# Joining levels 32 and 64 of a triangular inverse by small TensorE tiles ahead of a gated delta-rule recurrence

## The chip, the cores and the metric

The kernel runs on one core of one Trainium2 chip. The metric is the device time of one execution in microseconds (us): 2207.28 us is the median of three runs of the kernel before (2204.56, 2207.28 and 2207.43 us). TensorE is called PE here, its weight loads PEld, VectorE is DVE, ScalarE is ACT, GpSimd is POOL, SyncE is SP.

## What is computed

The reference is one decoder block on x of shape 4 x 512 x 512: a gated delta-rule attention with 16 heads of width 128, a cross attention and a routed low-rank feed-forward. The change is in the first of the three. Its core, cut to what matters:

```python
qkv = silu(causal_depthwise_conv(layernorm(x) @ Wqkv))   # 4 taps
q, k = l2norm(q), l2norm(k)
def step(M, inp):                      # M: a 128 x 128 state per batch and head
    q_t, k_t, v_t, b_t, g_t = inp
    M = M * exp(g_t)
    M = M + outer(k_t, (v_t - k_t @ M) * b_t)
    return M, q_t @ M                  # scanned over the 512 tokens
out = rmsnorm(out) * norm_w * silu(z) @ Wout
```

The kernel doesn't step through tokens. It takes chunks of 128 tokens. In a chunk, the corrections of all tokens are the solution of a system with a unit triangular 128 x 128 matrix, I + N, where N is strictly triangular and holds the products of keys with their decays. The output and the next state follow from this solution by plain matrix products. The change concerns how I + N is inverted and applied.

## The kernel before, in words

There are 16 heads, processed one after the other (the first and the last are unrolled, the 14 between are a loop). For each head there are 4 batches (B) and 4 chunks (NC), so 16 independent 128 x 128 systems. All five engines run one instruction stream each, in the order in which the code is written; semaphores are the only coupling. There is no scheduler.

A head goes through these stages on PE:

1. decays, transposes of k, and the gram products k k^T (L563 to L588);
2. the projections of q and z as 12 products of 128 x 512 each, "jobs" (L515), and the transposes of v and q;
3. the products k q^T (L635);
4. the inverse. The 16 x 16 diagonal blocks are inverted by POOL (`blkT`), and come back through DRAM into `t32`; DVE transposes them to `tT`. Then pairs of blocks are merged: with T the block diagonal inverse so far and X the off-diagonal blocks of N at that level, the update is T := T - T X T. It takes two products per system: `merge_y` (L670, X against T), a copy of its result from PSUM by ACT (L1086), `merge_z` (L683), and a subtraction by DVE (L1388). Level 0 goes from 16 to 32 and is followed by a 32 x 32 block transpose into `t32` (L1391). Level 1 goes from 32 to 64 and takes its X from `x1`, which ACT fills (L1024). Each level is four groups (one per chunk) of `merge_y` and four of `merge_z`, and a group is 4 matrix products of 128 x 128, one for each batch. A float32 product of this kind is two MATMUL records in the trace;
5. the recurrence over the chunks c = 0 to 3. The last level, 64 to 128, is never formed. It is applied: `w1` = T r (L708), `vv` = X2 w1 (L714), T vv (L719), and w = w1 - T vv by DVE (L1408). ACT copies in between (L1100, L1108). Then come the state product (L728) and the output products (L734, L735). For c > 0 there is first a product of the state with the keys (L702), which DVE subtracts from the right hand side (`nv`, L1400).

Into the waits of stage 5, `ahead(count)` puts products of the next head's first seven jobs (K for four batches, V for three), one 128 x 512 product each, by the table `FILL`: rows are chunks, columns are the places after L702, L708, L714 and L719. Two of the seven jobs are done before stage 4, the other 60 products are in `FILL`. Each finished job is scaled by ACT (`tap`, L954) and convolved by DVE in three steps (L1316), and a job may only begin when the convolution of the job before it in the same PSUM bank has ended. The convolution of V of batch 1 stands in DVE's order in chunk 3, ahead of `normalise` (L1328), whose result PE transposes (L554).

The last head has no next head; `ahead` does nothing there. ACT and DVE instead split the output weights in each chunk (L1128, L1429).

## Time and profile before

| | us |
|---|---|
| median of 3 runs | 2207.28 |
| span of the profiled execution | 2206.9 |
| PE busy | 2103.0 (95%) |
| PEld busy | 1734.9 (79%) |
| DVE busy | 1242.6 (56%) |
| ACT busy | 988.4 (45%) |
| POOL busy | 814.4 (37%) |
| mean granted TensorE clock | 0.989 |

The span runs from the first to the last instruction; the time of this execution around its span is not listed separately, and the span is 0.4 us under the median. A busy share of PE is not a share of its peak: matmuls are pipelined, so the duration of one record (277 ns for a 128 x 128 one) is longer than the distance from one to the next. Distances are read from the starts of groups in the timeline.

### The profile page before, as it was taken

The page shows a single profiled execution, that of the slowest core. Times are in us where ns is not written, and L with a number is a line of the kernel's source. Part 1 is how long each engine was busy: PE and PEld are TensorE (multiplying, and loading weights), DVE is VectorE, ACT ScalarE, POOL GpSimd, SP SyncE. Part 2 cuts the span into 40 slices and gives each one's busy share as a digit, 9 for nine tenths or more (in the row PEclk, how much of TensorE's full clock was granted, in tenths as well). Part 3 has the DMA queues.
Part 4 walks back from the last instruction along what each step waited for, and adds up shares of the span by engine and source line. Part 5 has one row for each costly group of instructions (what it writes and reads, how often), then busy time and mean ns, then how long its engine had stood idle before and what let it go on. Part 6 is the DMA issues. An engine that isn't in the chain of part 4 may idle for free.

```text
span 2206.9 us, 37731 instructions
## 1 busy us (share of the span) xinstructions
PE 2103.0 (95%) x12418; PEld 1734.9 (79%) x12418; DVE 1242.6 (56%) x2160; ACT 988.4 (45%) x3083; POOL 814.4 (37%) x1169
## 2 busy tenths in 40 slices
PE   5899999999999999999999999999999799999999
PEld 4688888888988888888888888888898665757574
DVE  5656565656666656566565656565666544343434
ACT  2455454546364646454555545464636331212111
POOL 2254453535353636353545445353535200000000
PEclk9899999999999999999999999999999989999999
DMA  2011111101010101010101111111102340403020
GB/s 93 15 34 26 29 36 21 31 21 35 22 38 14 38 19 38 14 38 15 37 21 31 29 24 36 21 31 21 36 21 63 125 128 10 115 16 109 19 57 19
DMA packets 220091, 85.37 MB, mean 39 GB/s; under 512 B 138320, under 2 KB 204240, under 8 KB 219280
## 3 DMA queue, kind: packets, MB, share of 16 engines
q1 hardware_dynamic: 220048, 84.83, 15.2%
q8 instruction: 23, 0.38, 0.1%
q14 instruction: 20, 0.16, 0.0%
HBM read 57.28 MB, written 27.53 MB: 38 GB/s over the span
## 4 chain that ended last, share of the span: by engine, by line
PE 72%; issue 12%; DVE 9%; ACT 3%; POOL 2%; DMA 1%; POOLq 0%; DVEq 0%; SPq 0%; ACTq 0%
PE bank L515 27%; PE bank L683 5%; PE bank L670 5%; PE bank L771 4%; PE bank L708 3%; PE bank L635 3%; PE bank L728 2%; PE bank L735 2%; PE bank L714 2%; PE bank L719 2%; PE bank L734 2%; PE bank L702 2%; DVE vT L1316 2%; PE bank L588 1%; PE bank L834 1%
## 5 line engine op out<-in xcount | busy, mean ns | idle before, releaser
L515 PE MATMUL bank<-x_hi,w_hi 128*128 128x512 f32 x1024 | 422.6, 413 | 18.3 <-DVE w_lo L1263 11.6
L515 PE MATMUL bank<-x_hi,w_lo 128*128 128x512 f32 x1024 | 409.5, 400 | 0.0
L515 PE MATMUL bank<-x_lo,w_hi 128*128 128x512 f32 x1024 | 408.5, 399 | 0.0
L515 PEld LDWEIGHTS bank<-x_hi,w_hi 128*128 128x128 f32 x1024 | 194.0, 189 | 60.0 <-issue 16.2
L515 PEld LDWEIGHTS bank<-x_hi,w_lo 128*128 128x128 f32 x1024 | 193.8, 189 | 36.7
L515 PEld LDWEIGHTS bank<-x_lo,w_hi 128*128 128x128 f32 x1024 | 194.5, 190 | 31.3
L1316 DVE SCALAR_TENSOR_TENSOR qT<-bank,cw,qT 128x511 f32<-128x511 f32 (+2 forms) x192 | 143.4, 747 | 82.7 <-ACT qT L954 78.1
L1316 DVE SCALAR_TENSOR_TENSOR vT<-bank,cw,vT 128x511 f32<-128x511 f32 (+2 forms) x192 | 143.2, 746 | 44.8 <-ACT vT L954 40.3
L1707 POOL TENSOR_TENSOR o_rstd<-o_ms,minus_half 128x4 f32<-128x4 f32 x64 | 70.7, 1104 | 258.1 <-DVE o_ms L1395 258.1
L1739 POOL TENSOR_TENSOR rstd<-ve,mhalf 128x1 f32<-128x1 f32 x32 | 17.4, 543 | 387.6 <-DVE ve L1479 387.6
L1114 ACT ACTIVATE o_tmp<-bank 128x128 f32<-128x128 f32 x256 | 67.4, 278 | 201.5 <-PE bank L735 201.5
L1316 DVE SCALAR_TENSOR_TENSOR kT<-bank,cw,kT 128x511 f32<-128x511 f32 (+2 forms) x192 | 142.6, 743 | 8.6 <-ACT kT L954 4.1
L1666 POOL TENSOR_TENSOR x<-nT,upper 128x512 f32<-128x512 f32 x64 | 84.8, 1335 | 142.9 <-PE bank L670 142.9
L1712 POOL TENSOR_TENSOR state<-state,gam 128x512 f32<-128x512 f32 x32 | 33.6, 1050 | 275.9 <-PE bank L735 275.9
L683 PE MATMUL bank<-tT,y 128*128 128x128 f32 x1024 | 134.8, 277 | 0.5 <-DVE tT L1388 0.5
L1408 DVE TENSOR_TENSOR w<-w,bank 128x512 f32<-128x512 f32 x64 | 43.8, 685 | 159.3 <-PE bank L719 159.3
L670 PE MATMUL bank<-t,x 128*128 128x128 f32 x1024 | 133.3, 276 | 0.0
L670 PEld LDWEIGHTS bank<-t,x 128*128 128x128 f32 x1024 | 124.4, 192 | 1.2
L683 PEld LDWEIGHTS bank<-tT,y 128*128 128x128 f32 x1024 | 124.2, 192 | 0.8 <-issue 0.7
L1086 ACT ACTIVATE y<-bank 128x512 f32<-128x512 f32 x128 | 76.5, 598 | 105.8 <-PE bank L670 105.8
L1388 DVE TENSOR_TENSOR tT<-tT,bank 128x512 f32<-128x512 f32 x128 | 87.2, 681 | 50.6 <-PE bank L683 50.4
L771 PE MATMUL bank<-wo_hi,o_hi 128*128 128x512 f32 x256 | 105.3, 412 | 0.0
(219 smaller groups left out, 4860.6 us busy)
## 6 DMA issues: line engine op xcount, KB each, us to landing
w_raw<-in_w_heads SPq DMA_DIRECT2D x64, 256.0 KB, 2.8
o_d<-og SPq DMA_DIRECT2D x64, 256.0 KB, 2.6
o_raw<-o_d SPq DMA_DIRECT2D x16, 1024.0 KB, 6.1
x_in<-in_x SPq DMA_DIRECT2D x16, 256.0 KB, 3.4
blkN_d<-nT SPq DMA_DIRECT2D x64, 64.0 KB, 2.0
t<-blkT_d SPq DMA_DIRECT2D x64, 64.0 KB, 2.4
wo_raw<-in_w_out SPq DMA_DIRECT2D x4, 1024.0 KB, 7.9
x_res<-in_x SPq DMA_DIRECT2D x16, 256.0 KB, 2.7
```

What stands on the lines that cost most here:

```text
L515: last = mm(bank[bk][:, :], w[:, kind % 2, d, :], xx[:, d, b * S:(b + 1) * S], start=(n == 0), stop=(n == 3 * ND - 1))
L635: last = mm(grid(5 + 2 * (c % 2))[:, b, :], kT[:, b, c, :], qT[:, b, c, :], start=True, stop=True)
L670: last = mm(grid(3 + n % 2)[:, b, :], x, t32[:, b, c, :], start=True, stop=True)
L683: last = mm(grid(5 + 2 * (n % 2))[:, b, :], y1[:, n % 2, b, :], tT[:, b, c, :], start=True, stop=True)
L708: last = mm(grid(3)[:, b, :], tT[:, b, c, :], nv[:, b, c, :], start=True, stop=True)
L771: last = mm(bank[c % 2][:, :], o[:, c % 2, k, :], w[:, k, :], start=(n == 0), stop=(n == 3 * H - 1))
L1086: fn(y1[:, n % 2, :, :], grid(3 + n % 2), ACT.Copy).then_inc(y_copied, 1)
L1114: last = fn(o_tmp[:, b, :], grid(4)[:, b, :], ACT.Square, accum_out=o_sq[:, c, b:b + 1])
L1316: stt(d[:, k:S], bank[JOB_BANK[JOBS.index((kind, b))]][:, 0:S - k], cw[:, kind, TAPS - 1 - k:TAPS - k], d[:, k:S], ALU.mult, ALU.add).then ...
L1388: tt(tT[:, :, c, :], tT[:, :, c, :], grid(5 + 2 * (n % 2)), ALU.subtract).then_inc(merged, 1)
L1666: tt(x0[:, (c + 1) % 2, :, :], nT[:, :, c, :], upper[:, :].unsqueeze(1).to_broadcast([P, B, P]), ALU.mult).then_inc(x0_done, 1)
L1707: tt(o_rstd[:, c, :], o_ms[:, c, :], minus_half[:, 0:B], ALU.pow).then_inc(orstd_done, 1)
```

## The change

Level 1 of the merges (8 groups of full products per head) and the two applied products of the recurrence (`vv`, T vv) are taken out. In their place stands a piece between the merges and the recurrence that completes the inverse in `tT`:

- `join32_y`, `join32_z`: 32 x 32 products that make the 64 x 64 inverses. `join32_y` has 16 products for each half g (two chunks), `join32_z` 24: two for `tT`, and a third whose transposed result goes to `t32`. Two tiles of the array alternate in them (j = 0 and 1), with results in different PSUM banks.
- `join64_y`, `join64_z`: 64 x 64 products, 8 per half each, that make the upper right 64 x 64 block of the 128 x 128 inverse.
- Copies from PSUM by ACT after the y parts and of the third product, and by DVE after the z parts.

In all there are 80 products of 32 x 32 and 32 of 64 x 64 per head. The recurrence then applies `tT` once (L708 before) and waits for `inverse_done`. `JOIN_FILL` puts 12 products of the next head into the joins, and `FILL` now has two places per chunk and 48 products. POOL no longer clears blocks of `nT` but one block of `t32`; ACT's filling of `x1` goes.

```diff
-FILL = ((0, 4, 4, 4), (7, 4, 4, 1), (6, 4, 4, 2), (6, 4, 4, 2))
+FILL = ((0, 6), (7, 7), (7, 7), (7, 7))
+JOIN_FILL = (4, 2, 3, 3)
+EARLY, LATE = slice(0, P // 2), slice(P // 2, P)
+FRONT = [slice(2 * j * PAIR, 2 * j * PAIR + PAIR) for j in range(2)]
+BACK = [slice(2 * j * PAIR + PAIR, 2 * j * PAIR + 2 * PAIR) for j in range(2)]
...
-    MERGES = 2 * NC
+    MERGES = NC
+    def front_bank(g, j):
+        return 3 + (g + j) % 2
+    def back_bank(g, j):
+        return 5 + 2 * ((g + j) % 2)
+    def half_bank(g):
+        return (2, 6)[g]
...
+                def join32_y(g):
+                    pe.wait_ge(t32_done, 4 * h + 2 * g + 2)
+                    pe.wait_ge(y_copied, MERGES * h + MERGES)
...
+                    for i in range(2):
+                        for b in range(B):
+                            for j in range(2):
+                                c = 2 * g + i
+                                last = mm(small(front_bank(g, j), BACK[j], i, b), nT[FRONT[j], b, c, BACK[j]],
+                                          t32[FRONT[j], b, c, FRONT[j]], start=True, stop=True)
+                    last.then_inc(y32_mm, 1)
+                def join32_z(g):
+                    pe.wait_ge(y32_done, 2 * h + g + 1)
+                    pe.wait_ge(merged, MERGES * h + MERGES)
...
+                            for j in range(2):
+                                mm(small(back_bank(g, j), FRONT[j], i, b), y32[BACK[j], c, b, :], tT[BACK[j], b, c, BACK[j]],
+                                   start=True, stop=True)
+                            last = mm(small(back_bank(g, 0), BACK[0], i, b), tT[BACK[0], b, c, BACK[0]], y32[BACK[0], c, b, :],
+                                      start=True, stop=True)
+                    last.then_inc(z32_mm, 1)
+                def join64_y(g):
+                    pe.wait_ge(z32n_done, 2 * h + g + 1)
...
+                            last = mm(large(half_bank(g), LATE, i, b), nT[EARLY, b, c, LATE], t32[EARLY, b, c, EARLY],
+                                      start=True, stop=True)
+                    last.then_inc(y64_mm, 1)
+                def join64_z(g):
+                    pe.wait_ge(y64_done, 2 * h + g + 1)
+                    pe.wait_ge(z32_done, 2 * h + g + 1)
...
+                            last = mm(large(half_bank(g), EARLY, i, b), y64[LATE, c, b, :], tT[LATE, b, c, LATE],
+                                      start=True, stop=True)
+                    last.then_inc(z64_mm, 1)
+                join32_y(0)
+                ahead(JOIN_FILL[0])
+                join32_y(1)
+                join32_z(0)
+                ahead(JOIN_FILL[1])
+                join32_z(1)
+                join64_y(0)
+                ahead(JOIN_FILL[2])
+                join64_y(1)
+                join64_z(0)
+                ahead(JOIN_FILL[3])
+                join64_z(1)
...
-                    pe.wait_ge(merged, MERGES * h + NC + c + 1)
+                    pe.wait_ge(inverse_done, 2 * h + c // 2 + 1)
...
                     last.then_inc(w1_mm, 1)
                     ahead(fill[1])
-                    pe.wait_ge(w1_done, 4 * h + c + 1)
-                    pe.wait_ge(x2_only, 2 * h + 2)
-                    for b in range(B):
-                        last = mm(grid(2)[:, b, :], nT[:, b, c, :], w1[:, c % 2, b, :], start=True, stop=True)
-                    last.then_inc(v_mm, 1)
-                    ahead(fill[2])
-                    pe.wait_ge(vv_done, 4 * h + c + 1)
-                    for b in range(B):
-                        last = mm(grid(3)[:, b, :], tT[:, b, c, :], vv[:, b, :], start=True, stop=True)
-                    last.then_inc(tv_mm, 1)
-                    ahead(fill[3])
...
+                def keep32_y(g):
+                    act.wait_ge(y32_mm, 2 * h + g + 1)
...
+                    for j in range(2):
+                        last = fn(y32[BACK[j], 2 * g:2 * g + 2, :, :], smalls(front_bank(g, j), BACK[j]), ACT.Copy)
+                    last.then_inc(y32_done, 1)
+                def keep32_n(g):
+                    act.wait_ge(z32_mm, 2 * h + g + 1)
+                    fn(t32[BACK[0], :, 2 * g:2 * g + 2, FRONT[0]].rearrange("p b c s -> p c b s"),
+                       smalls(back_bank(g, 0), BACK[0]), ACT.Copy, scale=-1.0).then_inc(z32n_done, 1)
+                def keep64_y(g):
...
                 for c in range(NC):
                     act.wait_ge(w1_mm, 4 * h + c + 1)
-                    fn(w1[:, c % 2, :, :], grid(3), ACT.Copy).then_inc(w1_done, 1)
+                    fn(w1[:, c % 2, :, :], grid(3), ACT.Copy).then_inc(w_done, 1)
                     if more and c == 3:
                         tap(h + 1, V_, 1)
...
-                    fn(vv[:, :, :], grid(2), ACT.Copy).then_inc(vv_done, 1)
...
+                def join32(g):
+                    dve.wait_ge(z32_mm, 2 * h + g + 1)
...
+                def join64(g):
+                    dve.wait_ge(z64_mm, 2 * h + g + 1)
+                    ts(tT[EARLY, :, 2 * g:2 * g + 2, LATE].rearrange("p b c s -> p c b s"), larges(half_bank(g), EARLY),
+                       -1.0, None, ALU.mult).then_inc(inverse_done, 1)
...
-                    dve.wait_ge(tv_mm, 4 * h + c + 1)
-                    tt(w1[:, c % 2, :, :], w1[:, c % 2, :, :], grid(3), ALU.subtract).then_inc(w_done, 1)
```

PE's order shows the two places of which the prediction speaks. The first is the start of the joins in the loop over the heads. Before, from the first `merge_y` of level 1 on, with the `merge_z` of one chunk behind each (`x_95` is `x1`, `y_96` is `y1`, `t_91` is `t32`):

```order
L670 MATMUL bank<-t_91,x_95 128x128 x4
L675 REGISTER_ALU
L683 MATMUL bank<-tT,y_96 128x128 x4
L670 MATMUL bank<-t_91,x_95 128x128 x4
L675 REGISTER_ALU
L683 MATMUL bank<-tT,y_96 128x128 x4
L670 MATMUL bank<-t_91,x_95 128x128 x4
L675 REGISTER_ALU
L683 MATMUL bank<-tT,y_96 128x128 x4
L670 MATMUL bank<-t_91,x_95 128x128 x4
L675 REGISTER_ALU
L683 MATMUL bank<-tT,y_96 128x128 x4
```

In the changed kernel the same place on PE, from the last `merge_y` (L701, `x_107` is `x0`) and the last two `merge_z` (L712) on; `y_104` is `y32`:

```order
L701 MATMUL bank<-t_91,x_107 128x128 x4
L712 MATMUL bank<-tT,y_96 128x128 x8
L733 MATMUL bank<-t_91,nT 32x32 x16
L570 ISA
L552 MATMUL bank<-x_hi,w_hi 128x512
L552 MATMUL bank<-x_lo,w_hi 128x512
L552 MATMUL bank<-x_hi,w_lo 128x512
L552 MATMUL bank<-x_hi,w_hi 128x512
L733 MATMUL bank<-t_91,nT 32x32 x16
L738 ISA
L748 MATMUL bank<-tT,y_104 32x32 x2
L750 MATMUL bank<-y_104,tT 32x32
```

Runs of small tiles and runs of full ones take turns: PE goes from one shape to another 11 times in a head with a next one (into `join32_y(0)`, into and out of each of the four fills, from 32 to 64 at `join64_y(0)`, and into the recurrence).

The second place is chunk 3 of the recurrence in the same loop. Before, from L708 to L719; two more L515 follow, and then the transposes L554 of the normalised output of chunk 2:

```order
L708 MATMUL bank<-nv,tT 128x128 x4
L515 MATMUL bank<-x_hi,w_lo 128x512
L515 MATMUL bank<-x_hi,w_hi 128x512
L515 MATMUL bank<-x_lo,w_hi 128x512
L515 MATMUL bank<-x_hi,w_lo 128x512
L714 MATMUL bank<-w_97,nT 128x128 x4
L515 MATMUL bank<-x_hi,w_hi 128x512
L515 MATMUL bank<-x_lo,w_hi 128x512
L515 MATMUL bank<-x_hi,w_lo 128x512
L515 MATMUL bank<-x_hi,w_hi 128x512
L719 MATMUL bank<-vv,tT 128x128 x4
```

And in the changed kernel, where L807 is what L708 was and L591 what L554 was:

```order
L807 MATMUL bank<-nv,tT 128x128 x4
L552 MATMUL bank<-x_hi,w_lo 128x512
L552 MATMUL bank<-x_hi,w_hi 128x512
L552 MATMUL bank<-x_lo,w_hi 128x512
L552 MATMUL bank<-x_hi,w_lo 128x512
L552 MATMUL bank<-x_hi,w_hi 128x512
L552 MATMUL bank<-x_lo,w_hi 128x512
L552 MATMUL bank<-x_hi,w_lo 128x512
L591 MATMUL bank<-ident,o_tmp 128x128 x4
```

Between these two, PE now has 7 fills; before it had 10 and two groups of full products. The orders of ACT (copy of `w1`, tap of V of batch 1, then tap of batch 2) and of DVE (`nv`, mean square, convolution of V of batch 1, `normalise`) in chunk 3 are as before but for the removed copy and subtraction.

## Rows read from the trace of the kernel before

**Rows 1.** Page: busy time of each engine, and the ending chain by engine

```profile
PE 2103.0 (95%) x12418; PEld 1734.9 (79%) x12418; DVE 1242.6 (56%) x2160; ACT 988.4 (45%) x3083; POOL 814.4 (37%) x1169
...
PE 72%; issue 12%; DVE 9%; ACT 3%; POOL 2%; DMA 1%; POOLq 0%; DVEq 0%; SPq 0%; ACTq 0%
```

**Rows 2.** Ending chain in order of time, two heads: start, us, what

```profile
902.05 0.93 PE bank L515 x4
...
928.39 0.23 PE bank L563
...
1033.18 0.23 PE bank L563
```

**Rows 3.** Timeline of PE, one head: start, us, instructions, idle before

```profile
985.29 1.06 PE L670 MATMUL bank<-t,x 128*128 128x128 f32 x8
986.18 1.06 PE L683 MATMUL bank<-tT,y 128*128 128x128 f32 x8
...
993.39 1.06 PE L708 MATMUL bank<-nv,tT 128*128 128x128 f32 x8
...
999.08 1.15 PE L728 MATMUL bank<-w,k_tok 128*128 128x128 f32 x8
...
1001.01 1.16 PE L702 MATMUL bank<-state,kdT 128*128 128x128 f32 x8
...
1003.83 1.16 PE L708 MATMUL bank<-nv,tT 128*128 128x128 f32 x8
...
1020.21 1.16 PE L728 MATMUL bank<-w,k_tok 128*128 128x128 f32 x8
...
1022.99 1.06 PE L702 MATMUL bank<-state,kdT 128*128 128x128 f32 x8
...
1025.27 1.05 PE L708 MATMUL bank<-nv,tT 128*128 128x128 f32 x8
...
1030.54 0.66 PE L554 MATMUL bank<-ident,o_tmp 128*128 128x128 f32 x4
...
1032.94 0.48 PE L563 MATMUL bank<-gt,after_r 128*128 128x512 f32 x1
```

**Rows 4.** Timeline of PE in the tail: full weights against 8 columns

```profile
1849.16 0.96 PE L831 MATMUL bank<-wg_sb,xfT 128*128 128x8 f32 x8
1849.97 2.39 PE L834 MATMUL bank<-a_sb,xfT 128*128 128x512 f32 x5
```

**Rows 5.** Timeline of DVE, the same head

```profile
1021.49 0.69 DVE L1418 TENSOR_TENSOR state<-state,bank 128x512 f32<-128x512 f32 x1 [0.45 <-PE bank L728]
1022.10 2.31 DVE L1316 SCALAR_TENSOR_TENSOR vT<-bank,cw,vT 128x511 f32<-128x511 f32 x3
...
1027.57 2.32 DVE L1316 SCALAR_TENSOR_TENSOR vT<-bank,cw,vT 128x511 f32<-128x511 f32 x3 [2.49 <-ACT vT L954]
1029.80 0.68 DVE L1328 TENSOR_TENSOR o_tmp<-bank,o_rstd 128x512 f32<-128x512 f32 x1
```

**Rows 6.** Timeline of ACT, the same head

```profile
986.88 0.61 ACT L1024 ACTIVATE x<-nT 32x128 f32<-32x128 f32 x2
...
1026.36 0.60 ACT L1100 ACTIVATE w<-bank 128x512 f32<-128x512 f32 x1 [0.98 <-PE bank L708]
1026.85 0.68 ACT L954 ACTIVATE vT<-bank,cw 128x512 f32<-128x512 f32 x1
```

**Rows 7.** Timeline of PE and ACT, last head

```profile
1721.34 1.06 PE L708 MATMUL bank<-nv,tT 128*128 128x128 f32 x8
...
1726.87 1.16 PE L728 MATMUL bank<-w,k_tok 128*128 128x128 f32 x8 [0.78 <-DVE w L1408]
...
1730.11 1.92 ACT L1128 ACTIVATE wo_hi<-wo_raw 128x2048 fp32r<-128x2048 f32 x1
...
1736.38 1.16 PE L728 MATMUL bank<-w,k_tok 128*128 128x128 f32 x8 [0.34 <-DVE w L1408]
```

**Rows 8.** Windows: one stretch with PE busy time, mean clock (PEclk)

```profile
1849.10:1850.10 1.00, 1.00 (x12) 1.00 (x10) 0.82 (x3) 0.91 (x2) 0.00 (x0) 1.00 0.00 0
```

More of the change, by code:

```diff
@@ new lines, in join32_z @@
+                def join32_z(g):
+                    pe.wait_ge(y32_done, 2 * h + g + 1)
+                    pe.wait_ge(merged, MERGES * h + MERGES)
+                    if g and not more:
+                        pe.wait_ge(z32_done, 2 * h + 1)
+                        pe.wait_ge(z32n_done, 2 * h + 1)
+                    hold(pe, "pe")
+                    for i in range(2):
+                        for b in range(B):
+                            c = 2 * g + i
+                            for j in range(2):
[4 more added lines that the diff above has]
+                    last.then_inc(z32_mm, 1)
```

157 lines of the change are left out of this document (83 added, 74 removed).

## The prediction

> **What bounds the kernel now.** I read the page first: PE is busy for 95% of the span, and 72% of the chain that ended last is PE's own work [rows 1]. So time taken from PE's stream counts, as long as no other engine becomes late. Then the chain in order of time gives the period: one head from L563 to L563 takes 104.8 us [rows 2], and 15 heads have a next head to fill in. One filled product costs 0.23 us (four in 0.93) [rows 2]. Then the timeline of PE through one head: a merge group starts 0.89 us after the one before it, so a full 128 x 128 float32 record takes 0.111 us of PE (8 in a group), though its duration reads longer [rows 3]. Last, DVE and ACT in chunk 3, where they are barely on time for PE [rows 5, 6].
>
> **The change, part by part, for a head with a next one.**
>
> (a) Level 1 of the merges goes. From the first level-1 group to L708 of chunk 0 there are 8.10 us [rows 3], and one group of 0.89 (the last `merge_z` of level 0) stays: minus 7.2 us.
>
> (b) The recurrence loses `vv` and T vv, two groups of about 0.92 with their hand-over, so 1.84 per chunk, and 12 fills of 0.23. What becomes late next decides how much of this is real.
> - Chunk 0: L708 to L728 takes 5.69 us now [rows 3]. Without 1.84 and six fills (1.38) it is 2.3 with ACT's copy (0.60) hidden by the fills: minus 3.4.
> - L728 of chunk 0 to L708 of chunk 1 is 4.75 us [rows 3]. DVE sets it (state copy, convolution, `nv`) and it stays.
> - Chunks 1 and 2 lose 1.84 each, and one and two fills net: minus 2.4 and minus 2.2. In the latter the last job must wait for DVE's convolution after the state sum: 0.61 + 2.31 after the sum begins, which is 1.28 after L728 [rows 3, 5], so at 4.2. PE has got there at 0.99 + 1.79 + 0.9 + 0.5 = 4.1 (L728 to L702 is 2.78 [rows 3]). A wait of 0.1.
> - Chunk 3 gains nothing. L708 to L554 takes 5.27 us [rows 3]. The path is not PE's: L708 to its end 1.06, ACT's copy, ACT's tap, DVE's convolution of 2.32, `normalise` of 0.68, then L554 [rows 3, 5, 6]. None of these moves. PE now has 0.85 + 7 x 0.23 = 2.5 us of work there, so it stands idle for 2.8 us where it had been covered by 1.84 + 0.69 more. L554 to the next head is 2.40 as before [rows 3].
>
> Sum: from L708 of chunk 0 to the next head 39.55 us now [rows 3], minus 3.4, 2.4 and 2.2: 31.5, minus 8.0 us.
>
> (c) The joins are added: 80 products of 32 x 32 and 32 of 64 x 64, two records each, so 160 and 64 records. No row has such a tile. The nearest is L831: 8 columns move, the loaded weights are 128 columns, and it still takes 0.81 us for 8 records, 0.10 each [rows 4], no less than with 128 columns. So the weight load sets the full-size record, and it could shrink with the columns: 28 ns (a quarter of 111) and 56 ns (half) are the lower bounds, and 111 ns is the upper bound for both, if a record costs the same whatever its tile. I take 50 ns for the small, between the bounds, nearer the lower since two tiles alternate, and 58 ns for the medium, close to the row scaled by its columns: 160 x 0.050 = 8.0 and 64 x 0.058 = 3.7.
>
> (d) Twelve fills move here: 2.8 us. Covers: ACT's two copies of 32 x 256 cost some 0.65 us (two of 32 x 128 took 0.61 [rows 6]); four fills (0.93) or a z part lie beside each. The first wait that is not covered is `join32_y(1)` for the last transpose on DVE: 0.1 us, and 0.7 if the small tiles are at their lower bound.
>
> (e) Eleven changes of tile shape. No row has one. Below: nothing. Above: the array runs empty, which is the duration of a 128 x 128 record less its distance; a group of 8 shows 1.06 for 0.89 [rows 3], so 0.17 each, 1.9. I take 0.07 each, 0.8, since a run of small tiles can begin beside the end of a full one.
>
> (f) Off the path: ACT loses `x1`, POOL its two memsets for a small one, DVE four subtractions in the merges and four in the recurrence. ACT and DVE take short PSUM reads instead. None of it is where PE waits. Nothing.
>
> Per head: minus 7.2, minus 8.0, plus 8.0 + 3.7 + 2.8 + 0.1 + 0.8 = 15.4, so plus 0.2 us; 15 heads: plus 3.
>
> **The last head** has no fills. Its joins are exposed: 8.0 + 3.7, 0.8 for the shapes, and a wait of about 1 us for copies, 13.5 against 7.2: plus 6.3. The recurrence gains more than elsewhere, since nothing covered the two copies: L708 to L728 was 5.53 [rows 7] and becomes 1.75 (1.06, 0.60 and two hand-overs). Between L728 of chunks 0 and 1 lay 9.5 [rows 7]; what remains is the output product, squares, ACT's split of 1.92 [rows 7] and the copy, 5.7: minus 3.8. The next two gain 3.5 each, with DVE's split of the output weights then near the path. Minus 14.6; net minus 8.
>
> Total: plus 3 minus 8 on a span of 2206.9 gives 2202; I say 2201 us, as the third figures don't carry. The median is 0.4 above the span, which changes nothing.
>
> **A rule against the change.** Nothing in these rows drains PE for a new shape. The Trainium skill, "TensorEngine Tiling (Array Packing)", Key Properties, says that a change of the tiling mode drains the engine, while tiles of one mode work in parallel. No row here shows either. The first is the third rival below, the second the first.
> The same page (Instruction Overhead) gives a matmul a cost of about 60 cycles however few columns it has. At 2.4 GHz that would be an estimate of 25 ns for each of a record's passes, in place of 28 ns by columns.
>
> **Rivals.**
>
> 1. The alternating tiles overlap fully, and a record costs its columns: 28 and 56 ns, shapes free. 4.5 + 3.6 + 2.8 + 0.7 = 11.6 per head instead of 15.4; minus 3.6 a head, minus 55, and minus 11 in the last: 2141 us. For it: distinct banks and partitions for j = 0 and 1. Against: only the 32 x 32 parts alternate.
>
> 2. A record costs nearly as much as a full one (fetching, starting and loading it), at the upper bound 111 ns: 160 and 64 of them are 24.9 us in place of 11.7. Plus 13.4 a head: some 2415. A related one: such thin work lets the granted clock fall. L831 ran at 1.00 with 8 columns [rows 8], but for under a microsecond. If the joins ran at half clock, their 11.7 and the fills' 2.8 would double: plus 14.5 a head, 2430; for half of the stretch, 2315.
>
> 3. The slower side, as one mechanism: at each change of shape PE runs empty and also can't load the new weights ahead. 0.17 for the drain and as much again for the load make 0.35; eleven are 3.9 in place of 0.8. Plus 3.1 x 16 = 50: 2251 us. It decides from 0.13 us per change on: 0.06 x 11 x 16 = 10.6 eats the 6 us and 0.2% more.
>
> 4. PE is not short of 2.8 us in chunk 3, if the tap of V there starts before ACT's copy. The order of ACT speaks against it. Minus 2.8 x 15 = 42: 2159.
>
> **How the numbers follow.** Forecast 0.31 (its own range 2180 to 2225, since 10 ns on the small record is 1.6 us a head, 26 in all), overlap 0.27, changes of shape 0.23, dear records or clock 0.16, chunk 3 0.03. Within 0.2% (4.4 us, about what a measurement can tell from no change) lies a third of the forecast: 0.10. Faster: 0.15 of the forecast, 0.27, 0.03 and a little of the others: 0.46. Slower: the rest, 0.44. The range for 8 in 10 runs from the overlap to the half-slow clock: 2140 to 2310.
>
> **What would show it.** In the changed profile: starts of the groups of 32 x 32, divided by 32 or 48 records (1.6 and 2.4 us expected; 0.9 and 1.3 by rival 1; 3.6 and 5.3 by rival 2). The distance from the last small record to the first fill against that inside a run (rival 3). The granted clock of the stretch. PE idle before the transposes of chunk 2's output in chunk 3, waiting for DVE's `normalise`, 2.8 us in each of 15 heads. From w1 of chunk 0 to the next head 31.5 us. I am wrong if a small record is outside 40 to 60 ns, if a change of shape takes over 0.13 us, or if that idle time is missing.

## The result, and the profile of the changed kernel

| | before | changed |
|---|---|---|
| median, us | 2207.02 (4 runs) | 2134.25 (4 runs, 2129.81 to 2136.12) |
| ratio, with 95% interval | | 0.967 (0.9656 to 0.9684) |
| profiled execution / its span | - / 2206.9 | 2134.65 / 2132.9 |
| mean granted TensorE clock | 0.989 | 0.980 |
| one head to the next, us | 104.7 mean | 99.4 in the shortest, 100.1 mean |

The changed kernel is 3.3% faster. The forecast was 2201 us, 0.3% faster, and its range ended at 2140. Its sign was right and its size was not.

The lines have moved: L563 is now L600, L515 is L552, L708 is L807, L728 is L817, L702 is L801, L554 is L591, ACT's `tap` L954 is L1043, DVE's convolution L1316 is L1404 and `normalise` L1328 is L1416. L733 is `join32_y`, L748 and L750 are `join32_z`, L764 is `join64_y`, L775 is `join64_z`.

The page (busy time by engine, then the ending chain by engine), to be held against [rows 1]:

```profile
PE 1988.0 (93%) x13954; PEld 1619.9 (76%) x13954; DVE 1201.4 (56%) x2128; ACT 928.9 (44%) x2955; POOL 790.2 (37%) x1152
...
PE 65%; issue 15%; DVE 15%; ACT 2%; POOL 2%; DMA 1%; DVEq 0%; POOLq 0%; ACTq 0%; SPq 0%
```

PE has 1536 records more and is busy for 115 us less. The chain has shifted from PE (72% to 65%) towards DVE and "issue": PE now waits at some places.

The joins of one head in PE's timeline (start, us, instructions, idle before). They stand where [rows 3] had the level-1 merges:

```profile
1046.26 2.01 PE L712 MATMUL bank<-tT,y 128*128 128x128 f32 x16
1048.20 0.69 PE L733 MATMUL bank<-t,nT 32*32 32x32 f32 x32
1048.82 0.50 PE L552 MATMUL bank<-x_hi,w_hi 128*128 128x512 f32 x1
...
1050.25 0.60 PE L733 MATMUL bank<-t,nT 32*32 32x32 f32 x27 [0.23 <-DVE t L1477]
...
1051.32 0.50 PE L552 MATMUL bank<-x_lo,w_hi 128*128 128x512 f32 x1
...
1052.61 1.14 PE L764 MATMUL bank<-t,nT 64*64 64x64 f32 x16
1053.68 0.50 PE L552 MATMUL bank<-x_hi,w_hi 128*128 128x512 f32 x1
...
1054.58 0.97 PE L764 MATMUL bank<-t,nT 64*64 64x64 f32 x13
...
1056.41 0.50 PE L552 MATMUL bank<-x_hi,w_hi 128*128 128x512 f32 x1
...
1057.30 1.14 PE L775 MATMUL bank<-tT,y 64*64 64x64 f32 x16
1058.37 1.16 PE L807 MATMUL bank<-nv,tT 128*128 128x128 f32 x8
```

Read the distances, not the durations. Thirty-two small records take 0.62 us (1048.20 to 1048.82). The next run of 80 takes 1.07 (1050.25 to 1051.32), and the last of 48 0.63 (1051.98 to 1052.61). That is 2.32 us for 160 records, 14 ns each, where 50 ns were forecast and 28 was the lower bound. The 64 medium records take 1.07, 1.83 and 1.07 us (the three rows of L764 and L775 with the next row's start), 62 ns each. Three fills take 0.90 (1053.68 to 1054.58) where three distances of 0.23 make 0.69, so each of the two changes of shape around them costs 0.10 at most, and less if the runs of small tiles give some of it back. With 0.1 taken off for the change at the end of each run, the small record is 13 ns and the medium 57. From the first small record to L807 there are 10.2 us.

The recurrence after it runs from L807 at 1058.37 to the next head's L600 at 1089.42 in the same timeline, 31.05 us. The end of it, as PE and then DVE show it (timelines of chunk 3, to be held against [rows 3, 5]); the first fence is PE one head earlier, the second DVE:

```profile
987.85 0.63 PE L591 MATMUL bank<-ident,o_tmp 128*128 128x128 f32 x4 [2.66 <-issue]
...
990.02 0.48 PE L600 MATMUL bank<-gt,after_r 128*128 128x512 f32 x1
```

```profile
1084.23 2.32 DVE L1404 SCALAR_TENSOR_TENSOR vT<-bank,cw,vT 128x511 f32<-128x511 f32 x3 [2.95 <-ACT vT L1043]
1086.47 0.68 DVE L1416 TENSOR_TENSOR o_tmp<-bank,o_rstd 128x512 f32<-128x512 f32 x1
```

PE stands idle for 2.66 us before L591, behind the convolution and `normalise`, as forecast (2.8). The waits of PE over the whole span (us, times, longest):

```profile
PE bank L591 <- issue: 42.2, 18, 2.7
```

Something was not forecast: after that idle time the clock falls. The head that begins at 688.06, again PE's timeline, and the windows (length, PE busy, PEld, DVE, ACT, POOL, clock, DMA, GB/s):

```profile
685.18 0.63 PE L591 MATMUL bank<-ident,o_tmp 128*128 128x128 f32 x4 [2.66 <-issue]
...
688.06 0.77 PE L600 MATMUL bank<-gt,after_r 128*128 128x512 f32 x1
```

```profile
688.00:692.00 4.00, 4.00 (x21) 3.43 (x21) 2.36 (x5) 3.53 (x15) 1.99 (x4) 0.75 0.24 66
990.00:994.00 4.00, 4.00 (x27) 3.48 (x26) 2.89 (x6) 3.67 (x17) 2.11 (x4) 1.00 0.22 66
```

The same L600 reads 0.77 us at one head and 0.48 at another. In the slower one the granted clock was 0.50 (1.2 GHz) for some 3 us. This happens behind 8 of the 15 idle times of 2.66 us; the fall begins while PE is still idle or up to 1.4 us after it has gone on. Before, every head start had 1.00.

Where the time went, from the starts of the heads: 15 periods were 1570.5 us and are 1501.7, minus 68.7. Fifteen times the shortest period (99.37) would be 1490.6, so a gain of 79.9 was there and some 11 of it is given back by the clock. The part ahead of the first head is 2.0 shorter, which need not be the change's doing: that part varies between 89.2 and 91.6 us over the kernels of this document. The part from the last head's start on is 3.4 shorter. The sum is minus 74.1 on the span.

### The profile page after: what moved, and what is told of

It is laid out like the page before. It is cut to its first block, busy times and chain, and to the rows that moved or that the text cites. A ratio compares the mean times of both kernels' runs of the same rounds, so it can differ in the third digit from the quotient of the medians.

```text
span 2132.9 us, 40248 instructions
## 1 busy us (share of the span) xinstructions
PE 1988.0 (93%) x13954; PEld 1619.9 (76%) x13954; DVE 1201.4 (56%) x2128; ACT 928.9 (44%) x2955; POOL 790.2 (37%) x1152
## 4 chain that ended last, share of the span: by engine, by line
PE 65%; issue 15%; DVE 15%; ACT 2%; POOL 2%; DMA 1%; DVEq 0%; POOLq 0%; ACTq 0%; SPq 0%
PE bank L552 28%; PE bank L860 4%; DVE kT L1404 3%; PE bank L807 3%; PE bank L672 3%; PE bank L824 3%; PE bank L823 2%; DVE t L1477 2%; PE bank L801 2%; PE bank L817 2%; DVE tT L1475 2%; DVE tT L1466 2%; PE bank L764 2%; PE bank L775 2%; PE bank L625 1%
## 5 line engine op out<-in xcount | busy, mean ns | idle before, releaser
L552 PE MATMUL bank<-x_hi,w_hi 128*128 128x512 f32 x1024 | 425.1, 415 | 20.2 <-DVE w_lo L1351 11.9
L552 PE MATMUL bank<-x_lo,w_hi 128*128 128x512 f32 x1024 | 404.9, 395 | 0.0
L552 PE MATMUL bank<-x_hi,w_lo 128*128 128x512 f32 x1024 | 404.9, 395 | 0.0
L552 PEld LDWEIGHTS bank<-x_hi,w_hi 128*128 128x128 f32 x1024 | 193.0, 188 | 70.8 <-issue 16.4
L552 PEld LDWEIGHTS bank<-x_hi,w_lo 128*128 128x128 f32 x1024 | 192.7, 188 | 39.8
L552 PEld LDWEIGHTS bank<-x_lo,w_hi 128*128 128x128 f32 x1024 | 193.5, 189 | 31.4
L1404 DVE SCALAR_TENSOR_TENSOR qT<-bank,cw,qT 128x511 f32<-128x511 f32 (+2 forms) x192 | 143.4, 747 | 83.4 <-ACT qT L1043 78.9
L1404 DVE SCALAR_TENSOR_TENSOR vT<-bank,cw,vT 128x511 f32<-128x511 f32 (+2 forms) x192 | 143.2, 746 | 51.5 <-ACT vT L1043 47.0
L1404 DVE SCALAR_TENSOR_TENSOR kT<-bank,cw,kT 128x511 f32<-128x511 f32 (+2 forms) x192 | 142.6, 743 | 7.9 <-ACT kT L1043 3.4
L860 PE MATMUL bank<-wo_hi,o_lo 128*128 128x512 f32 x256 | 99.9, 390 | 0.0
L860 PE MATMUL bank<-wo_lo,o_hi 128*128 128x512 f32 x256 | 99.9, 390 | 0.0
L1460 DVE TENSOR_TENSOR pT<-bank,pT 128x512 f32<-128x512 f32 x64 | 44.2, 691 | 98.6 <-PE bank L672 98.6
L1733 POOL TENSOR_TENSOR pT<-pT,cvec 128x512 f32<-128x512 f32 x64 | 67.1, 1049 | 85.2 <-DVE cvec L1435 82.4
L824 PE MATMUL bank<-w,pT 128*128 128x128 f32 x512 | 96.8, 288 | 0.0
L1194 ACT ACTIVATE w<-bank 128x512 f32<-128x512 f32 x64 | 38.2, 598 | 125.6 <-PE bank L807 125.5
L1351 DVE TENSOR_TENSOR w_lo<-w_raw,w_hi 128x512 fp32r<-128x512 f32 x64 | 53.5, 836 | 68.2 <-ACT w_hi L1019 68.2
```

The source lines that it names most:

```text
L552: last = mm(bank[bk][:, :], w[:, kind % 2, d, :], xx[:, d, b * S:(b + 1) * S], start=(n == 0), stop=(n == 3 * ND - 1))
L824: last = mm(grid(4)[:, b, :], pT[:, b, c, :], w1[:, c % 2, b, :], start=(c == 0), stop=True)
L860: last = mm(bank[c % 2][:, :], o[:, c % 2, k, :], w[:, k, :], start=(n == 0), stop=(n == 3 * H - 1))
L1351: tt(w_lo[:, kind % 2, :, :], w_raw[:, kind % 2, :, :], w_hi[:, kind % 2, :, :].bitcast(F32), ALU.subtract).then_inc(wlo_done, 1)
L1404: stt(d[:, k:S], bank[JOB_BANK[JOBS.index((kind, b))]][:, 0:S - k], cw[:, kind, TAPS - 1 - k:TAPS - k], d[:, k:S], ALU.mult, ALU.add).then ...
L1460: tt(pT[:, :, c, :], grid(5 + 2 * (c % 2)), pT[:, :, c, :], ALU.mult).then_inc(pT_done, 1)
```

## The experiments

Three theories were put to the test, each with its opposite. Overlap: the small record is cheap because two tiles take turns (against: it is cheap by its few columns alone). Clock: thin work by itself lowers the granted clock (against: only idle time does). Chunk 3: the idle time there comes from the order of work on ACT and DVE and can be taken away (against: something else holds PE up next). The letters in the expectations mean what each of them says.

### e3_one_tile: the same products, one tile after the other

```diff
-                    for i in range(2):
-                        for b in range(B):
-                            for j in range(2):
+                    for j in range(2):
+                        for i in range(2):
+                            for b in range(B):
```

`join32_z` is turned in the same way, its three kinds of product one after the other.

> The changed kernel with the 32 x 32 products in another order: all of one tile of the array, then all of the next, instead of alternating. The number of products is the same. Theory A (the 13 to 16 ns come from neighbouring tiles working at the same time; one tile alone takes its columns, 28 ns a record): 160 x 13 ns = 2.1 us a head more, 2134 + 33 = 2167 us at most, and runs of 32 records of L733 that last 0.9 us in place of 0.5. Rival B (a record of 32 columns costs 14 ns whatever its neighbour): 2134, runs as long as before.

Measured: 2265.54 us (2265.16 to 2265.97), ratio 1.0265 (1.0248 to 1.0282). PE's timeline, and three windows of 4 us from 905.30 on:

```profile
903.33 1.09 PE L733 MATMUL bank<-t,nT 32*32 32x32 f32 x32
904.36 0.50 PE L552 MATMUL bank<-x_hi,w_hi 128*128 128x512 f32 x1
...
909.88 1.97 PE L767 MATMUL bank<-t,nT 64*64 64x64 f32 x16
911.78 0.79 PE L552 MATMUL bank<-x_hi,w_hi 128*128 128x512 f32 x1
```

```profile
905.30:909.30 4.00, 4.00 (x119) 3.41 (x118) 0.83 (x2) 1.13 (x3) 0.00 (x0) 1.00 0.00 0
909.30:913.30 4.00, 4.00 (x41) 3.12 (x38) 0.83 (x2) 0.97 (x2) 0.00 (x0) 0.55 0.00 0
913.30:917.30 4.00, 4.00 (x35) 3.73 (x35) 0.60 (x1) 0.59 (x1) 0.52 (x1) 0.50 0.00 0
```

The first 32 records take 1.03 us in place of 0.62 at the same clock. Without the 0.1 for the change of shape behind them that is 29 ns each against 16. So the record is cheap because different tiles take turns. The total is not explained by it: the clock goes to 0.50 about 6 us into the joins and stays there for some 14 us, and all heads but the first take 108.4 to 109.3 us. The expectation had no term for that, and missed by 100 us.

### e2_small_twice and e4_medium_twice: each product issued twice

```diff
                         for b in range(B):
-                            for j in range(2):
...
+                            for _ in range(2):
+                                for j in range(2):
...
```

```diff
-                            last = mm(large(half_bank(g), LATE, i, b), nT[EARLY, b, c, LATE], t32[EARLY, b, c, EARLY],
-                                      start=True, stop=True)
+                            for _ in range(2):
+                                last = mm(large(half_bank(g), LATE, i, b), nT[EARLY, b, c, LATE], t32[EARLY, b, c, EARLY],
+                                          start=True, stop=True)
```

> The changed kernel with every 32 x 32 product issued twice in a row (160 records more per head; the second one writes the same result). Theory A (a small record costs 13 to 16 ns of PE, tiles overlapping): 2.1 to 2.6 us a head, less up to 0.5 that lies in the wait for DVE's last transpose: 2134 + 16 x 1.7 to 2.5 = 2161 to 2174 us. Rival B (50 ns each, as predicted, with the present gain from elsewhere): 2134 + 16 x 8 = 2262. Rival C (the records' time is hidden behind waits for ACT and DVE): no change, 2134.

> The changed kernel with every 64 x 64 product issued twice in a row (64 records more per head, 56 ns each by the starts in the trace). Theory A: 3.6 us a head, 2134 + 16 x 3.6 = 2191 us (somewhat more if the slow clock of the last head doubles it there). Rival (a record of the same tile behind another is cheaper since the weights are the same): under 2170.

Measured: medium twice 2196.72 us (2196.1 to 2201.35), 62.5 above the changed kernel. That is 3.9 us a head for 64 more records, 61 ns each, near the 58 of the forecast. The medium term stands. The last head, at its lower clock, is part of this mean; the shortest periods, 103.10 against 99.37, give 58.

Small twice took 2334.14 us (2333.56 to 2336.9), 200 above the changed kernel and far from every expectation. The record alone doesn't do it; in the timeline of the joins 64 of them run in 1.13 us, 18 ns each:

```profile
941.52 1.20 PE L734 MATMUL bank<-t,nT 32*32 32x32 f32 x64
```

A head takes 110 to 116 us. The clock is at 0.50 for 10 to 17 us of it, in and after the joins, and in most heads again around the head's start. Besides, PE waits with no releaser in the trace, among the small products (L750) and at the head's start (L619, and L600 with 8.3 us in 13 waits); together with one wait of 2.6 these make 53 us:

```profile
PE bank L750 <- issue: 23.5, 22, 1.7
PE bank L619 <- issue: 18.6, 13, 1.9
```

What these waits stand behind can be seen in the DMA queue that the page names "instruction": it holds 159 packets of 16 KB here and 26 in the changed kernel. This is taken up at e9_full_extra. How the 200 us divide between records, waits and clock was not measured one by one.

### e6_one_tile_filled: one tile, with more full products between the joins

Against e3_one_tile:

```diff
-FILL = ((0, 6), (7, 7), (7, 7), (7, 7))
-JOIN_FILL = (4, 2, 3, 3)
+FILL = ((0, 6), (6, 6), (6, 6), (6, 6))
+JOIN_FILL = (6, 4, 4, 4)
```

> The changed kernel with the 32 x 32 products one tile after the other (as in e3_one_tile) and 18 instead of 12 filled products in the joins (JOIN_FILL 6, 4, 4, 4; FILL 0, 6 and then 6, 6 three times). It tells apart the two costs in e3's extra 131 us. Theory A (28 ns a record for a tile by itself, 2.1 us a head; the rest of e3 was the granted clock, which fell in the joins because too little full-size work lay between the small runs): the clock stays at 1.00 and the time is 2134 + 33 + some 10 for waits in the chunks with fewer fills = 2165 to 2185. Rival B (the clock falls by the thin work itself, whatever lies between): 2250 or more, clock 0.93 as in e3.

Measured: 2211.34 us (2208.83 to 2211.83, 10 runs), ratio 1.0016 (1.0007 to 1.0026). It lies between the two expectations, 54 us below e3_one_tile. The joins now hold their clock in all 15 heads that have a next one, where e3_one_tile lost it in 14; the end of the head, of which six fills were taken away, does not. Windows of the joins (13.60 us) and of the end of the same head:

```profile
988.60:1002.20 13.60, 13.60 (x243) 11.41 (x242) 4.25 (x8) 3.44 (x8) 0.70 (x2) 1.00 0.00 0
```

```profile
1031.10:1035.10 4.00, 3.06 (x21) 3.09 (x21) 3.07 (x6) 0.00 (x0) 0.00 (x0) 0.77 0.04 12
```

PE's waits show what else the moved fills cost: 27.3 us in 32 waits for the convolution of k, which now is late in chunk 1.

```profile
PE bank L552 <- DVE kT L1407: 27.3, 32, 5.8
```

A head takes 104.95 us in the mean, against 100.1. Of these 4.8 some 2.1 are the order of the records, 1.4 is this wait, and 0.5 two shorter ones (for the convolution of V, and the idle time before L591, now 2.87). The clock falls at the end of 11 of the 15 heads in place of 8. Its share was not taken apart; it lies in the 0.8 that is left. What follows: with more full products among them the same small records, at the same cost, no longer lower the clock.

### e9_full_extra: nine more full products in the joins of the changed kernel

```diff
+                def extra(count):
+                    if more:
+                        pe.wait_ge(conv_done, 12 * (h + 1) + conv_index(K_, 1) + 1)
+                        for _ in range(count):
+                            mm(bank[1][:, :], w_hi[:, K_ % 2, 0, :], x_hi[:, 0, 0:S], start=True, stop=True)
                 join32_y(0)
+                extra(3)
                 ahead(JOIN_FILL[0])
```

Two more stand ahead of each of the other three `ahead`. Their results are not used.

> The changed kernel with nine more 128 x 512 products per head between the joins' small runs (in 15 heads, into a bank that is free there; nothing reads their result): 9 x 0.23 = 2.1 us a head, the same extra time as e3_one_tile's records, but full-width work. Theory A (e3's fall of the clock comes from thin work, not from a longer stretch): clock as in the changed kernel, 2134 + 15 x 2.1 less what lies in the 0.23 us wait = 2162 to 2168 us. Rival (a longer stretch of joins is what makes the clock fall): well over 2200.

Measured: 2181.03 us, with 10 runs from 2168.28 to 2204.2, ratio 0.9886 (0.9853 to 0.9918). The fastest run lies at the expectation's end; the median is 13 above it. The trace shows two things on top of nine products of 0.23 us. The clock falls at the head's start again (a head is 102.45 us, where 99.37 and 2.08 make 101.45), so full work in the joins doesn't guard against the idle time of chunk 3. In the joins of these heads it holds, so a longer stretch is not what lowered it in e3_one_tile. And at four heads PE waits for 1.7 to 3.5 us before the first product of a head, with no releaser:

```profile
506.20 0.76 PE L600 MATMUL bank<-gt,after_r 128*128 128x512 f32 x1 [3.48 <-issue]
```

That wait is neither in the kernel before nor in the changed one. In the kernel with the small products twice it is there as well. The traces show what goes with it. The queue named "instruction" on the page, of this kernel between 400 and 505 us and of e2_small_twice over the whole span (packets, MB, share):

```profile
q8 instruction: 9, 0.15, 0.7%
q8 instruction: 159, 2.61, 0.5%
```

In the changed kernel this queue brings 12 packets in the first two heads and then none until the end of the fifteenth. Here it goes on through the sixth head, and the four waits stand exactly at the starts of the third to the sixth; from 700 to 1600 us there is no packet and no such wait. In e2_small_twice and e12_norm_small_twice it brings 8 to 13 packets in every head, and every head has such waits: in e12, a packet is on its way from 370.94 to 372.11, and PE stands idle from 372.21 to 373.64. So these are waits of PE for its instructions, as far as the traces tell; no run took the packets away by themselves. Why the loop needs them again in these kernels is open: e4_medium_twice has more PE records in a head than this one, and no packet between its second head and its last two. The four waits are 11.0 us of this execution. Whether they are also the wide spread is not shown, since one execution was profiled.

### e1_tap_first: the tap of V ahead of the copy of w

In chunk 3, ACT reads the finished projection of V before it copies `w1`.

```diff
+                    if more and c == 3:
+                        tap(h + 1, V_, 1)
                     fn(w1[:, c % 2, :, :], grid(3), ACT.Copy).then_inc(w_done, 1)
-                    if more and c == 3:
-                        tap(h + 1, V_, 1)
```

> The changed kernel with one edit: in chunk 3 ACT does the tap of V of batch 1 ahead of its copy of w1. Theory A (PE's idle 2.66 us ahead of the transposes L591 in 15 heads is the chain w1 - ACT copy - tap - DVE convolution - normalise, and the falls of the granted clock at 8 of the head starts follow from that idle time): the idle time goes, the clock stays at 1.00 at every head start, the heads become 96.7 us long, 15 x 2.66 = 40 us plus some 11 us of slow clock: about 2084 us. Rival B (the clock falls because the small tiles are thin work): the idle time goes but the falls stay: about 2094. Rival C (another wait, POOL's or DVE's, takes the place at once): 2125 or more.

Measured: 2095.26 us (2093.96 to 2096.6), ratio 0.9491 (0.9475 to 0.9506), 39.0 less than the changed kernel. Heads take 97.4 us, all alike, and each begins at a clock of 1.00. The idle time before L591, of PE over the whole span:

```profile
PE bank L591 <- issue: 12.8, 18, 0.8
```

ACT, DVE and PE at that place, each from its timeline:

```profile
863.30 0.64 ACT L1019 ACTIVATE w_hi<-w_raw 128x512 fp32r<-128x512 f32 x1
863.83 0.70 ACT L1043 ACTIVATE vT<-bank,cw 128x512 f32<-128x512 f32 x1
```

```profile
864.56 2.32 DVE L1404 SCALAR_TENSOR_TENSOR vT<-bank,cw,vT 128x511 f32<-128x511 f32 x3 [0.99 <-ACT vT L1043]
```

The tap stands behind two other pieces of work of ACT (the silu of k and the split of w), so it comes at 863.83 and DVE still waits 0.99 for it. Fifteen times 1.97 us make 30, and with the clock's 11 that are no longer lost 41; 39 were measured. The expectation of 2084 had taken all of the idle time away; 0.71 of it stays. Behind that shorter idle time the clock falls in none of the 15 heads.

### e7_norm_first: and `normalise` ahead of the convolution

On top of e1_tap_first, in DVE's chunk 3:

```diff
+                        normalise(h, c - 1)
                         if more and c == 3:
                             conv(h + 1, V_, 1)
-                        normalise(h, c - 1)
```

> The changed kernel with two edits in chunk 3: ACT's tap of V of batch 1 ahead of its copy of w1 (as in e1_tap_first, 2095 us), and DVE's normalise of chunk 2 ahead of the convolution of that V. Theory: e1's remaining idle time of 0.71 us ahead of L591 is normalise behind the convolution; it goes, and nothing else moves up: 2095 - 15 x 0.7 = 2085 us. Rival (the convolutions end later, and DVE is late at the next head's start, at k_sqe and k_tok): 2095 or more.

Measured: 2081.54 us (2080.07 to 2082.99), ratio 0.9429 (0.9413 to 0.9445). Heads take 96.5 us, and no wait before L591 is left in them. PE's timeline in chunk 3, the seventh fill and what follows it:

```profile
859.99 0.39 PE L552 MATMUL bank<-x_hi,w_lo 128*128 128x512 f32 x1
860.21 0.60 PE L591 MATMUL bank<-ident,o_tmp 128*128 128x128 f32 x4
```

That is 3.5 us under the 2085 expected. From the chunk 3 idle time alone, the two edits take 2.8 us a head and the clock's fall: 52.7 us of 2134. The idle time is caused by the order in which ACT and DVE do their work, and is not needed.

### e11_norm_one_tile and e12_norm_small_twice: the clock without the idle time of chunk 3

On e7_norm_first, the edit of e3_one_tile and that of e2_small_twice:

```diff
...
-                            for j in range(2):
...
+                    for j in range(2):
...
```

```diff
...
+                            for _ in range(2):
...
```

> The kernel is e7_norm_first (2081.5 us, heads of 96.5 us, clock 1.00 at every head start) with the small products in the order of e3_one_tile. Two readings of e3_one_tile, which was 131 us slower than the changed kernel and lost its clock in the joins: (A) the thin one-tile joins lower the granted clock by themselves; then it falls here too, and the same 131 us come on top, 2190 to 2225 us, with a clock of 0.50 in the later part of the joins; (B) the clock fell only because PE had also stood idle in chunk 3 before, and without that idle time it stays at 1.00: then only the records cost more, 160 x 13 ns = 2.1 us per head, 33 us in all, 2105 to 2125 us. A at 0.55, B at 0.45.

> The kernel is e7_norm_first with each 32 x 32 product issued twice, as in e2_small_twice, which was 200 us slower than the changed kernel. (A) the thin joins lower the clock by themselves: again about 200 us on top, 2250 to 2300 us; (B) with no idle time in chunk 3 the clock holds: 160 more records at 14 ns, 2.2 us, and some 1.5 us of the waits without a releaser that e2_small_twice showed between the small products, 3.7 us per head, 60 us in all, 2125 to 2155 us. The z parts will show whether those waits (1.44 us at the longest) are there at full clock too.

Measured: one tile 2175.13 us (2172.64 to 2184.34), ratio 0.9868 (0.9845 to 0.989); small twice 2303.57 us (2293.66 to 2309.21), ratio 1.0426 (1.0394 to 1.0458).

For small twice, A's number nearly holds (its range ended 4 us lower): the clock falls in the joins of every head with a next one, for 10 to 17 us. It is not a test of A's reason, though, since PE waits with no releaser in the joins of each of these heads, for 1.2 to 1.7 us, and the fall comes 0.5 to 3.7 us after that wait begins.

One tile is the clean test: from 926 us to the end of the joins of that head no wait of PE over 0.03 us is in the trace. It lies between A and B, and its heads tell why. Seven of them take 97.4 to 98.65 us, eight take 106.0 to 106.1, nearly in turns. The short ones are 96.54 plus 2.08, which is B's price. That it is B's to the tenth is partly luck: the runs of small records are 2.4 us longer in these joins, 15 ns for each of 160, and some 0.3 of that lies in the wait of 0.23 before the second `join32_y`, which is gone. The long ones have the clock at 0.50 for about 17 us in and after the joins: A's fall, 7.45 us more. Eight times 7.45 and fifteen times 2.08 are 91 of the 94 measured. The windows of two heads in a row (868.00 in the first and 966.60 in the second are both 59.2 us behind the head's start):

```profile
868.00:872.00 4.00, 4.00 (x89) 3.14 (x87) 1.36 (x4) 1.88 (x5) 0.00 (x0) 1.00 0.00 0
872.00:876.00 4.00, 4.00 (x78) 3.48 (x78) 1.13 (x3) 0.97 (x2) 0.00 (x0) 1.00 0.00 0
...
966.60:970.60 4.00, 4.00 (x88) 3.14 (x88) 1.35 (x4) 1.88 (x5) 0.00 (x0) 1.00 0.00 0
970.60:974.60 4.00, 4.00 (x66) 3.82 (x65) 1.10 (x3) 0.37 (x1) 0.00 (x0) 0.54 0.00 0
974.60:978.60 4.00, 4.00 (x30) 3.25 (x30) 0.00 (x0) 1.02 (x2) 0.32 (x1) 0.50 0.00 0
```

PE's records fill these windows (4.00 of 4.00) where the clock falls. So the busy time of the profile doesn't tell whether the clock will hold; the same code holds it in one head and not in the next.

The Trainium skill, "TensorE: Matmul & The Clock Gate", HAM oscillation, ties a falling clock to waits between bursts of matmuls. The trace agrees in chunk 3, where the idle time of 2.66 us, shorter than the waits of the page's case, stands before the fall and its removal cures it. It doesn't agree in the joins of the one-tile kernel, where no wait stands before it.

In small twice the waits between small products come at full clock too, ahead of the fall. PE in the joins, where the window from 932.80 to 936.80 has a clock of 0.96:

```profile
934.46 0.22 PE L750 MATMUL bank<-tT,y 32*32 32x32 f32 x2 [1.44 <-issue]
```

### e10_best: the best version

On e7_norm_first, the convolution of k is moved between `join32` and `join64` on DVE, and the last head, which has no fills, gets full products in their place, with a result that is not used:

```diff
+                def keep_warm(count):
+                    if not more:
+                        for _ in range(count):
+                            mm(bank[0][:, :], ident[:, :], nT[:, 0, :, :], start=True, stop=True)
                 join32_y(0)
+                keep_warm(3)
                 ahead(JOIN_FILL[0])
```

Two, one and one of them stand at the other three places. On DVE `join64` has the moved convolution ahead of it:

```diff
-                    conv(h + 1, K_, 1)
...
+                if more:
+                    conv(h + 1, K_, 1)
```

> e7_norm_first with two more edits: DVE's convolution of K of batch 1 moves from ahead of the merges to between join32 and join64 (it frees the wait of 0.23 us ahead of the second join32_y in each head), and in the last head, where nothing fills the joins, seven float32 products of 128 x 512 whose result nobody reads lie in the waits for DVE and ACT, so that the granted clock need not fall there. Theory: 15 x 0.3 = 4 us for the first; for the second the clock stays at 1.00 from the joins on, 5 to 7 us less the products that are not in a wait (2 us): 2085 - 8 = 2077 us. Rival: the clock of the last head falls all the same, and the filler only costs: 2082 to 2085.

Measured: 2078.26 us (2077.77 to 2079.08), ratio 0.9417 (0.9402 to 0.9433). This beats both kernels: 5.8% under the one before, 2.6% under the changed one. In the last head the clock stays at 1.00 in every window from 1580 to 1615 us, where without these products it is at 0.50 from about 1594 on; from the last head's start to the end it takes 539.6 us in place of 542.75. The windows at that place, of e7_norm_first and of this kernel:

```profile
1594.00:1598.00 4.00, 2.88 (x117) 2.71 (x112) 1.59 (x4) 1.50 (x4) 0.00 (x0) 0.50 1.02 426
```

```profile
1595.00:1600.00 5.00, 4.68 (x76) 2.71 (x75) 1.26 (x4) 1.28 (x3) 0.00 (x0) 1.00 0.66 241
```

The moved convolution did nothing that can be told: the wait of 0.2 before `join32_y(1)` is still there, and a head is 96.50 in place of 96.54.

## Why the prediction was wrong

| step, per head | forecast | measured |
|---|---|---|
| (a) level 1 goes | -7.2 | gone, as read |
| (b) w1 of chunk 0 to the next head | 31.5 us (-8.0) | 31.05 us (-8.5) |
| (c) 160 small records | 8.0 (50 ns) | 2.0 (13 ns) |
| (c) 64 medium records | 3.7 (58 ns) | 3.7 (57 ns); 3.9 in e4 |
| (d) fills and wait | 2.8 + 0.1 | 2.8 + 0.2 |
| (e) eleven changes of shape | 0.8 (0.07 each) | up to 1.1 (0.10 each) |
| not assigned | | 0.4 |
| joins in sum | 15.4 | 10.2 |
| head | +0.2 | -5.4 at full clock, -4.6 in the mean |
| last head, to its last output product | -8 | -4.9 (-3.4 at the end of the span) |

**The failed step is (c), "I take 50 ns for the small".** The joins came out 5.2 us shorter than forecast; the small record alone accounts for 6.0, and the wait, the shapes and what is not assigned give 0.8 back. The upper bound was worth nothing: the row for it (8 moving columns with a full load, [rows 4]) showed what a 128-column load costs, and I took a value between that and the columns, though two tiles in different rows of the array take turns in the order. The lower bound, 28 ns, was a bound only for one tile after the other. That is what e3 and e11 measure (27 to 29 ns); with different tiles in turn the record costs about half (e11's joins: 15 ns less a record, with nothing else changed). The starts of single records in the changed kernel say how. Records of one tile start 31 to 32 ns apart, with two tiles in turn as within a run of one; a record of another tile starts mostly 6 to 7 ns behind its neighbour, inside that time. Two tiles in `join32_y` make 16 ns a record. The three products of `join32_z` go to three tiles, and a round of three takes as long as a round of two (PE's timeline, a round and the start of the next):

```profile
1052.10 0.20 PE L748 MATMUL bank<-tT,y 32*32 32x32 f32 x2
1052.11 0.19 PE L750 MATMUL bank<-y,tT 32*32 32x32 f32 x1
1052.13 0.20 PE L748 MATMUL bank<-tT,y 32*32 32x32 f32 x2
```

Sixteen such rounds take 0.51 us (1051.98 to 1052.49), 11 ns a record. e3 and e11 changed the order of PSUM banks together with that of the tiles. The rounds of three speak against the bank, and against the rows of the array, as the cause: the third product has the bank and the input rows of the first and another tile, and starts 13 ns behind it; the next round's first follows it after 18 ns, not 31. No run changed the bank alone.

The time was therefore also under the first rival's, whose joins were 11.6 us against 10.2 measured. The mark that the prediction had set itself, a small record outside 40 to 60 ns, was met.

The Trainium skill, "TensorEngine Tiling (Array Packing)", Key Properties, says that different tiles work in parallel; 13 ns against 28 agrees. It also says that a change of mode drains the engine; up to 0.10 us for each change is in line with that. Its Instruction Overhead of about 60 cycles would be an estimate of 25 ns for each pass; records of different tiles start 6 to 7 ns apart here, under it, and those of one tile 31 to 32, above it.

**(b) and the idle time were right.** That PE would stand idle before the transposes in chunk 3 was read from the orders of ACT and DVE: 2.8 forecast, 2.66 measured. The stretch of (b) came out 0.45 us shorter than forecast. That this was also the cheapest thing left to mend was not seen; rival 4 had only asked whether it would mend itself.

**The clock was a rival, and not a term.** It was priced for the joins, at 0.16, and stayed away there in the heads with a next one. It fell after the idle time of chunk 3 instead, in 8 of 15 heads, some 11 us in all. The forecast named the idle time and did not ask what it does to the clock.

**The last head** gained 4.9 us up to its last output product where 8 was forecast, though its small records were cheap. Its joins took 12.0 us for 13.5, and the recurrence behind them gained 10.4 for 14.6. With no fills among the joins the clock falls there. Timeline and window of PE:

```profile
1646.15 0.60 PE L733 MATMUL bank<-t,nT 32*32 32x32 f32 x27 [1.36 <-DVE t L1477]
...
1649.03 3.78 PE L764 MATMUL bank<-t,nT 64*64 64x64 f32 x32
```

```profile
1650.00:1655.00 5.00, 4.97 (x48) 4.89 (x47) 0.46 (x1) 1.18 (x2) 0.52 (x1) 0.50 0.52 182
```

Medium records cost twice the 57 ns there (3.53 us for 32 from 1649.03 to the 1652.56 of the next group), and what follows is slow until about 1663. Of the 4.2 us that the recurrence fell short, some 2.6 are not lost in e10_best, where the clock holds; the other 1.6 are the forecast's own, most of it since each of the later chunks gains 3.0 where 3.5 was forecast.

**Rivals.** The first had the right mechanism, overlap, with 0.27, and its 2141 us was 7 off. That is partly luck: its joins were 1.4 us too long in each head, and the clock and the last head took most of that back. Its sum is also not what it says: 11.6 for 15.4 is 3.8 a head and 57 in all, not 3.6 and 55, and with these its 2141 comes out. The second, dear records, is refuted for the changed kernel; its clock half is what e3 and e11 showed, and near its size: 7.45 us in a head of e11, where the 2315 us for half of the stretch had meant 7.1. The slow stretch is another one, though; it begins 5 us into the joins and runs past them. The third, 0.35 a change, is refuted by 0.10. The fourth didn't happen by itself; done by hand it is worth 52.7 us.

## What to carry to other kernels

For small tiles, ask first whether neighbours in the order are different tiles of the array: turning a loop halved the cost of a record here, and the wrong order cost another 7.45 us in each head in which the clock then fell. Where a change speeds up one engine, list every place where it now waits for another, and look at the order of work on that other engine: two swaps took back 2.8 us a head here. Look at the granted clock at the places with waits and with thin work, window by window, since the busy time doesn't show it. Where PE waits with no releaser, look at the page's instruction queue.

## What the hardware did that was not expected

- Float32 records of one 32 x 32 tile start 31 to 32 ns apart, and those of different tiles mostly 6 to 7 ns. So a record costs PE 16 ns with two tiles in turn, 11 with three, and 27 to 29 with one tile after the other (e3, e11; less than 31, since records of the two tiles overlap where one gives way to the next).
- A change of the tile's shape costs up to 0.10 us, the same between 32 and 128 (e6: 6 fills in 1.59 us, 989.65 to 991.24) and between 64 and 128.
- The granted clock falls to 0.50 in joins in which PE has no idle time (e11, 970.6 to 978.6), stays there for about 17 us, and does so in one head and not in the next with the same code. With more full products among the small ones it stays at 1.00 (e6, e10).
- An idle time of 2.66 us is followed by a fall in 8 of 15 heads, one of 2.87 (e6) in 11 of 15, one of 0.71 (e1) in none.
- PE waits with no releaser in the trace, up to 1.7 us between small products and up to 3.5 us at the start of a head (e2, e9, e12), and only in heads in which the instruction queue brings packets of 16 KB.
